# A masked softmax of four cross-attention layers: both halves of the last layer's mask on VectorE, and a new order of work

## The chip, the core and the metric

One core of a Trainium2 chip runs the whole program in one launch. The metric is the device time of that launch in microseconds (us), the median of several runs. Five engines take part: TensorE (PE in the profile, with its weight loads as PEld), VectorE (DVE), ScalarE (ACT), GpSimd (POOL) and SyncE (SP), which here only starts transfers. Matrix products land in PSUM, in banks of 512 float32 per partition. GpSimd touches no bank in this kernel, so that whatever it works on has been brought to SBUF by VectorE or ScalarE first.

## The reference

32 sequences of 64 rows by 256 pass through four attention layers. The last one has a self-attention (called C in the kernel), a cross-attention (F) and an MLP (H); its masked scores are what the change is about.

```
def attention(q, k, v, mask):
    scores = jnp.einsum('bhqd,bhkd->bhqk', q, k) / jnp.sqrt(jnp.float32(HD))
    scores = scores * mask - 10000.0 * (1.0 - mask)
    probs = jax.nn.softmax(scores, axis=-1)
    return jnp.einsum('bhqk,bhkd->bhqd', probs, v)
...
ctx = merge_heads(attention(split_heads(q), split_heads(k), split_heads(v), ltor_mask))    # C
x = hidden_states + ctx @ w_ao + b_ao
...
ctx = merge_heads(attention(split_heads(q), split_heads(k), split_heads(v), cross_mask))   # F
x = x + ctx @ w_co + b_co
x = x + gelu(layernorm(x, ln3_s, ln3_b) @ w1 + b1) @ w2 + b2                               # H
```

The mask acts in two halves: a factor (mask / 4, since the head size is 16) and a summand (10000 * mask - 10000). There are 16 heads of 64 by 64 scores for each sequence.

## The kernel before

Two sequences share the 128 partitions, so there are 16 pairs (index i). Each pair passes through stages with letters: N, Q, A and D are the first layer (norm, queries, scores with softmax, transposes and values), K the projections of the context, B the second layer, E and G the third layer's attention and MLP, C, F and H the fourth layer. W are products of a constant tile with itself whose result nobody reads. They keep TensorE at work: WARM_UP of them at the head of the program, IDLE_WORK at its end, once the last pair has left the first layer. S is the setup.

Every stage is a generator for each engine (`pe_c`, `dve_c`, `pool_c` and so on). The table ORDER holds one string for each engine; each letter advances that stage's generator by one step, and `weave` writes the program out in that order. The order of every engine's queue is thus fixed ahead, letter by letter, and pairs overlap: while one is in A, others are in B to H. BANK gives, in the order of TensorE's fills, which of 7 banks each fill uses. `fill_bank` makes TensorE wait until the bank's last user has released it (semaphore free), `wait_fill` makes a reader wait for the fill (full), and `release` marks the instruction that frees the bank.

An attention of C or F goes so. TensorE fills four banks with a quad of heads each (L684, 256 columns of a bank). VectorE multiplies each by the factor, from the bank into the SBUF tile p (L1170 in C, L1219 in F), which releases the bank. GpSimd adds the summand in SBUF, for 8 heads at a time (`pool_attention`, L824), two instructions for one stage. VectorE then takes the maximum (L754), subtracts it (L759), ScalarE raises to the exponential (L788), TensorE transposes (L698), VectorE sums (L763), and the product with the values follows (L711). B and E mask in another way and aren't touched. GpSimd's other large work is scaling the first layer's probabilities (L587) and spreading keys (L815).

Of the kernel before, what the change touches and what calls it, by code (L numbers as in the profile page):

```python
# [10 lines left out]
ALU = mybir.AluOpType  # L11
# [4 lines left out]
NSEQ, S, D = 32, 64, 256  # L16
# [46 lines left out]
WARM_UP = 32  # L63
IDLE_WORK = 68
# [18 lines left out]
def transpose_fills():  # L83
    fills = []
    for u, j, n in units():
# [24 lines left out]
        "nkbsssbnssssfnssskndsnfbedndnkednnebknybfdnneefkfnenekydybbnbnekfkfdydnnkbynefnkbddnynenkfdykdffeybnbnednnkdfn"  # L110
        "ybkyfnbennbeefbkydnfkfeydyyyy"),
    "pe": (
        "wwwwwwwwwwwwwwwwwwwwwwswwwknwsnkswwwwwwqqnasnaakkkskdkddadndddaaddsdnsddaaddddqddqaadddkkdkddnanadbkdbddbndddd"
        "adadddbbabdndbaekeeddeeddqddddqaddekebeenanaedbebaddkgdkggndddggbbaabdcdbncecedccdddaadedecdcdcecdqqddfaddfdfd"
        "eeeenanbefbfdefdkkfkaagkkgddgkhgngbdddkhhckhhcccbbacbdddnbaddeaacececdddcedeqddfddddfqfddeeeebnaanefbfefdkdkka"
        "agfkgdggngdddbadhdcdkhndkcchccbkbabddcbkehecaaceddcddeheddqfddddfqfddeebeenanefafefbkfkkaagkkkggnddgghbdhkkhdc"
        "hnhcbccbddcabddddbaddeaaddeecdcdececqqddfddddfdfdeeeebanenafefbaafgkgdfgkkggnhkkdhbddkhckkcccddcadbhdbddabddcn"
        "hbddceaaceecddeeddfdddfdqfddeebeeanqebffaafedkfkkangkkgbdggngdhdkhhcbnhcccbhcddbaaddbkdkecdcddaacedecddededddf"
        "dddfqfddqneeeeaneffafbekfkkbdaagdkgggdgdkkbddhnkckhchchchacdbbdddnbaddcbcdeaaceeddcdeeddqfdddfdafddqneebeednae"
        "fbfefdkkagfdgkgkdknggbddaahkkhchndddbccdbcbddcadbkhhcedcaaceedcededddfdddfqfddqeeeennaefbfefbkfkkaaakkgkgdgdgh"  # L120
        "dnghbdkkchnccchddcabbddbddbhcceaddaacdededcededdfdddfdqfddqeeeenaeffnfebkkkaagbkfnkggdbdgkdgdhkaddchbckcbhchha"
        "cbddddbaddnccaaeddecdedeceqddfdddfdfddqnebeeeanaefbfefdkkfkagkkngbdkggnhgadhcdkccbchbcddbaadhchdbcddekddaacdee"
        "ddcdeeddfddddfdfqqdeeebenanaebffedfdkkfgaakgghndkggbdkhcnhckkcbcbddcaabdhbdhedkcdcddaacdedecddeeddfdddfdqfddee"
        "beeaqnebffefanaagkfgkdgdkgkghbddknkkhchcnccbddbcaabdhbhdedcdkcddaacedddedceeddqqdfdddfddfebenneebefafefkkfkaaa"
        "kdgkgdgdhggkhbdkchcccddcaabhhdbkcddcdbcbddecaaedfedfdfdeeddddddfffkkddkeebkbefebwwekhehhgkbbgbgbgegeeewwweckcc"
        "chkcweeewehwecwwecwwwcwwgcggfggfwwfwwwcwwwccwwwfccfwwwfkfcwwcwwwcwwwwchwwwhfwwwfwwfhhhffwwwwfwwwwfwwwwwwwwwwwh"
        "wwwhhhh"),
# [12 lines left out]
    "dve": (  # L140
        "nnsknkknnknnnsnnnsnasansaaskaksfaaakndanadnanaaandnsdaanasnananankddaaabkaakakddaaadnaaannanakdadbbbbbabbdbbab"
        "bdbannneaananaabadbnnaaeendaneaeeeeeddaeadekeaenaannaneaaegbgggbbbgdbbkbkabbdangnbbgbagnacccakcndabnbcanacadec"
        "cnakeccccaaccecnccadcdaacnecfeffaeefeeadfdaffefeefdnfeffaffeffafeagfdgkgngfhahgaahnhknagagkdnabgncccbnbebcbnbb"
        "hhkbbkabbbfchcacccadcncadaabccacacnccacneennacakdacffdfeeaefeekedfdeffeffdefefnaafffaefffaaegngkfggdbgannaaakf"
        "gagahnhhgdachnnccbbbcbnbabdfabnbhdbcbcbkabhncceccnccaacccbccanecakanckadkeackaffdaffeeeeedehfdeffdfeefefnfafff"
        "efffakengfagaggfaghhaakanangfangkhdbenhgabcnbbbbnbcckhcbhbbbnbnabhdncccccakacckddcabancaccaaadeccecaadnaceecff"
        "feaefebeddfeffdfefefeafknfafefaaegffggfgangaafagnkfahegnhhahagcnfcknchbbabdbbcbkbhbckbcdbbccbcakcadcncdnccckan"
        "aahcnnbckncnaaadceaaeacfdfafeefeeedfedffedfefefafeffnfaefffbaaaefagkgagfghhgankeaangbabhbnbgbbhbbngnbcccncnbhd"
        "bbdahckcncchccccaacncbnaaadnckcdacncakaeckafaaedcfaffdefeeeedfedffeffeefnffefnkfffdfaeakfaaeggfageghgaafahagdg"
        "hbnankgdcckahcbbbbncbnbbbnbkhahbcncbbhacccacdccdcancaacbccnacnananckeaeadcafdkffaeefeeeedfdaaffffedeanefffekff"  # L150
        "ffefaaegggfgnagdankfhaghghnedbkhgabbbcnbcbcbbcabnkbnabnbhbaanhacddacccnccaccnabcncchkccnacfkadaeceaakcafdffaee"
        "feeedfedfffefeefdffkeffnffenfaakefgaggngfaahgakabahnkghhgaannanndgcccbhbfcdbbknahbcbbcbkbnebbbcccacnccdccabcdc"
        "cncaaahnaaacedaaeakcfdfkfaeefeeedfedffefefefeffffnffdfaenkaegggfggaananknafbaghghbabbbbhbbnkhgcddcacbcbbfbaaeb"
        "kakhchcnnhaccccadcdccacabnacccacanadnbnenkaaecdakcfffeeaefeeefddffeffdefenffaaenffaefffaeagfgggknfgahnaakhhngb"
        "abbbbbnhgnknnbbdfngcccbcahebbdccabcchccnaccacnccccahcdbndaaakkakaaceaeaadcfffdbaefeeeedfefdffefdeeffneafaffafe"
        "kffaaeggggfngkfanahahdhngahgnkaangnabccbcnbbcbbdbbbbnhbbcchkecnfccacacaacdbccaccdnnkcncaahacbeaaeacdffdfkaefee"
        "eedfedffedffeefafeffffeffakegnggagafagnaakafhkhhggdaaahkngbcncbcbnnnbnbbcbbbdfbaehbccnkhbccnacccaccbaancdccabd"
        "cnhcknaaakeaacdeadckfffaeeeeefeeddfedfffefeeffefkfffeffkanafnegfahggaagegkahaahgahdgagccafchbcbdbbbhbcbcbbbkcc"
# [102 lines left out]
def build(nc, dram, out):  # L261
    ctx = ExitStack()
    with ctx:
# [897 lines left out]
        def dve_c(i):  # L1161
# [7 lines left out]
            def masked(ps, dst):  # L1169
                return dve.tensor_tensor(dst, ps, bc(self_mul[:, :], 1, HB // 2), ALU.mult)  # L1170
# [399 lines left out]
```

## Time and profile before

| | us |
|---|---|
| median of 3 runs | 1190.07 |
| the 3 runs | 1190.07, 1185.77, 1190.25 |
| the profiled execution's own time | 1190.05 |
| its span | 1188.3 |
| PE busy | 1177.5 (99%) |
| DVE busy | 943.5 (79%) |
| ACT busy | 843.8 (71%) |
| POOL busy | 636.4 (54%) |

The profile was taken in one execution. Its own time is 1.75 us above its span, for what lies before the first and behind the last instruction. "Busy" of PE counts matmuls whose ends are modelled, so that a busy PE also holds small pauses between groups. A time in the sections below is counted from the start of the span.

### The profile page before, as it was taken

What the parts mean: (1) busy time and instruction counts of PE and PEld (TensorE: products, weight loads), DVE (VectorE), ACT (ScalarE), POOL (GpSimd) and SP (SyncE); (2) the same over time, 40 slices, a digit from 0 to 9 for tenths busy, and PEclk for the clock granted to TensorE, in tenths of its full rate; (3) what the DMA queues carried; (4) which work ended last, traced back from release to release, by engine and by line L of the source; (5) the groups of instructions that cost most, each with busy time, mean ns of one, the idle gap of its engine ahead of it and who ended that gap; (6) DMA issues with size and microseconds to landing.
All of it is one profiled execution on the core that took longest, in us unless ns stands there. A gap on an engine that the chain in (4) does not pass through costs nothing.

```text
span 1188.3 us, 35233 instructions
## 1 busy us (share of the span) xinstructions
PE 1177.5 (99%) x13192; PEld 973.2 (82%) x13192; DVE 943.5 (79%) x2282; ACT 843.8 (71%) x2273; POOL 636.4 (54%) x1003
## 2 busy tenths in 40 slices
PE   9999999999999999999999999999999999999998
PEld 8777788887887879888787887878888787888887
DVE  4788787978878787787969788797887979788764
ACT  3777786776777677687777868677686776866543
POOL 1654664646465464645656466464654555373341
PEclk8999999999999999999999999999999999999999
DMA  7400000000100000010000000010000100000000
GB/s 240 153 19 29 2 26 12 28 3 7 30 7 20 18 20 14 7 31 7 26 1 11 27 17 25 1 34 6 8 21 1 28 16 2 13 6 2 1 6 10
DMA packets 27623, 27.90 MB, mean 23 GB/s; under 512 B 11073, under 2 KB 25409, under 8 KB 26817
## 3 DMA queue, kind: packets, MB, share of 16 engines
q1 hardware_dynamic: 26240, 24.99, 6.9%
q8 instruction: 109, 1.79, 0.6%
q10 hardware_dynamic: 1216, 0.66, 0.3%
q14 instruction: 58, 0.47, 0.1%
HBM read 23.53 MB, written 2.10 MB: 22 GB/s over the span
## 4 chain that ended last, share of the span: by engine, by line
PE 95%; DVE 2%; ACT 1%; issue 1%; POOL 0%; POOLq 0%; ACTq 0%; DVEq 0%
PE bank L540 10%; PE bank L660 10%; PE attended L615 10%; PE bank L952 10%; PE bank L600 10%; PE bank L962 9%; PE bank L698 6%; PE bank L666 6%; PE bank L725 5%; PE bank L684 4%; PE bank L711 4%; PE bank L511 3%; PE bank L653 3%; PE bank L434 2%; PE attended L1255 2%; PE bank L716 1%
## 5 line engine op out<-in xcount | busy, mean ns | idle before, releaser
L587 POOL TENSOR_SCALAR p_a<-p_a,rec_a 128x256 f32<-128x256 f32 x512 | 246.0, 495 | 121.3 <-DVE rec_a L561 117.9
L576 ACT ACTIVATE p_a<-bank,nmax_a 128x256 f32<-128x256 f32 x512 | 237.3, 475 | 48.8 <-DVE nmax_a L555 47.8
L555 DVE TENSOR_REDUCE nmax_a<-bank 128x2 f32<-128x512 f32 x256 | 170.4, 679 | 15.3 <-PE bank L540 14.0
L600 PE MATMUL bank<-ident,p_a 128*128 128x128 f32 x1024 | 143.0, 275 | 0.3 <-POOL p_a L587 0.2
L540 PE MATMUL bank<-cc,q_a 64*128 64x256 f32 x1024 | 133.0, 390 | 0.4
L600 PEld LDWEIGHTS bank<-ident,p_a 128*128 128x128 f32 x1024 | 116.2, 142 | 17.2 <-issue 10.8
L615 PE MATMUL attended<-p_a,v_a 128*64 128x256 f32 x1024 | 125.8, 386 | 0.2 <-DVE p_a L633 0.2
L540 PEld LDWEIGHTS bank<-cc,q_a 64*128 64x128 f32 x1024 | 93.6, 186 | 24.6 <-issue 12.9
L576 ACT ACTIVATION_READ_ACCUMULATOR p_a<-bank,nmax_a 128x1 f32 x512 | 105.6, 206 | 0.0
L615 PEld LDWEIGHTS attended<-p_a,v_a 128*64 128x64 f32 x1024 | 67.2, 136 | 43.5 <-issue 14.6
L633 DVE COPY p_a<-bank 128x512 f32<-128x512 f32 x128 | 86.3, 679 | 7.3 <-PE bank L600 6.8
L648 ACT ACTIVATE p_a<-bank 128x512 f32<-128x512 f32 x128 | 75.7, 599 | 20.9 <-PE bank L600 20.2
L952 PE MATMUL bank<-h_xnT,wc 128*128 128x128 f32 x512 | 62.2, 276 | 0.5 <-ACT h_xnT L907 0.5
L952 PE MATMUL bank<-g_xnT,wb 128*128 128x128 f32 x512 | 61.7, 276 | 0.0
L952 PEld LDWEIGHTS bank<-h_xnT,wc 128*128 128x128 f32 x512 | 59.9, 192 | 1.7 <-ACT h_xnT L907 1.2
L952 PEld LDWEIGHTS bank<-g_xnT,wb 128*128 128x128 f32 x512 | 59.7, 192 | 0.8 <-ACT g_xnT L907 0.2
L962 PE MATMUL bank<-wc,h_hid 128*128 128x256 f32 x256 | 59.8, 380 | 0.0
L962 PE MATMUL bank<-wb,g_hid 128*128 128x256 f32 x256 | 59.7, 381 | 0.0
L523 ACT ACTIVATE q_a<-bank,bq 128x512 f32<-128x512 f32 x64 | 42.3, 686 | 24.0 <-PE bank L511 23.8
L844 POOL TENSOR_TENSOR b_p<-b_p,b_rec 128x512 f32<-128x512 f32 x32 | 33.6, 1053 | 46.3 <-DVE b_rec L766 46.3
L1136 POOL TENSOR_TENSOR e_p<-e_p,e_max 128x1024 f32<-128x1024 f32 x26 | 49.2, 1901 | 13.4 <-DVE e_max L754 13.3
L824 POOL TENSOR_TENSOR c_p<-c_p,self_add 128x512 f32<-128x512 f32 x32 | 41.8, 1311 | 20.0 <-DVE c_p L1170 19.9
(262 smaller groups left out, 2893.5 us busy)
## 6 DMA issues: line engine op xcount, KB each, us to landing
xx<-in_x SPq DMA_DIRECT2D x32, 128.0 KB, 2.8
cc<-in_ctx SPq DMA_DIRECT2D x32, 128.0 KB, 2.7
wc<-in_wc SPq DMA_DIRECT2D x3, 1024.0 KB, 12.1
k_c<-in_ctx SPq DMA_DIRECT2D x16, 128.0 KB, 2.3
wb<-in_wb SPq DMA_DIRECT2D x2, 1024.0 KB, 6.2
res_a<-in_x SPq DMA_DIRECT2D x16, 128.0 KB, 2.4
out<-y_out SPq DMA_DIRECT2D x16, 128.0 KB
wb<-in_wb SPq DMA_DIRECT2D x2, 512.0 KB, 4.9
```

Of the source, the lines that this page charges most:

```text
L540: ins = mm(bs[e][:, qt * D:(qt + 1) * D], q_a[rows_, j, n, qt * P:(qt + 1) * P], cc[rows_, z, n, :], start=True, stop=True)
L555: dve.tensor_reduce(nmax_a[:, n, e, :], ps[:, :].rearrange("p (q k) -> p q k", q=KT), AX.X, ALU.max, negate=True).then_inc(A.s["max"], 1)
L576: last = act.activation(p_a[:, j % 2, n, e, qt, :], ps[:, qt * D:(qt + 1) * D], ACT.Exp, bias=nmax_a[:, n, e, qt:qt + 1], accum_out=sum_a[ ...
L587: last = pool.tensor_scalar(p_a[:, j % 2, n, e, qt, :], p_a[:, j % 2, n, e, qt, :], rec_a[:, n, e, qt:qt + 1], 1.0, ALU.mult, ALU.mult)
L600: last = nc.tensor.transpose(ps[:, kt * D + qt * P:kt * D + (qt + 1) * P], p_a[:, j % 2, n, e, qt, kt * P:(kt + 1) * P], ident[:, :])
L615: last = mm(attended_bank[n * S:(n + 1) * S, 0:D], v_a[:, n, kt, h * S:(h + 1) * S], p_a[:, j % 2, n, e, kt, :], start=h == 0 and kt == 0, ...
L633: release(A, dve.tensor_copy(p_a[:, j % 2, n, 1, :, :], ps[:, :].rearrange("p (k q) -> p k q", k=KT)), i, ("x", u, 1))
L648: release(A, act.activation(p_a[:, j % 2, n, 0, :, :], ps[:, :].rearrange("p (k q) -> p k q", k=KT), ACT.Copy), i, ("x", u, 0))
L660: last = mm(ps[:, m * P:(m + 1) * P], w[:, k, m * P:(m + 1) * P], srcT[:, k, :], start=k == 0, stop=k == KT - 1)
L666: last = mm(ps[:, 0:D], srcT[:, k, :], w[:, k, :], start=k == 0, stop=k == KT - 1)
L952: last = mm(ps[:, m * P:(m + 1) * P], W["w1"][:, k, cols_], T.xnT[:, k, :], start=k == 0, stop=k == KT - 1)
L962: last = mm(ps[:, 0:D], T.hid[:, m, :], W["w2"][:, m, :], start=m == 0, stop=m == MT - 1)
```

## The change

In C and F, VectorE now does both halves. For each quad it multiplies the bank by the factor and writes the result back to the same place in the bank (line 746 of the changed kernel), raising a semaphore `weighed`; then it adds the summand, from the bank into SBUF (L1167 in C, L1215 in F), and this second instruction releases the bank. The product of the next quad is written ahead of the sum of this one. GpSimd's addition is gone, and the maximum waits for the release of the bank, where it waited for GpSimd before.

```
-RAISED_C = {"res": 1, "madd": KT, **SOFTMAX, **NORM}
+RAISED_C = {"res": 1, "weighed": QUADS, **SOFTMAX, **NORM}
...
-        def dve_attention(T, i, masked, dst):
+        def dve_attention(T, i, masked, dst, weight=None):
             dve, blocks = nc.vector, T.blocks
             for g in range(QUADS):
                 yield
+                if T in (C, F):
+                    for later in range(g, min(g + 2, QUADS)) if g == 0 else range(g + 1, min(g + 2, QUADS)):
+                        yield
+                        ps = wait_fill(T, dve, i, ("s", later))
+                        scores = ps[:, 0:D].rearrange("p (h k) -> p h k", h=HB // 2)
+                        dve.tensor_tensor(scores, scores, bc(weight[:, :], 1, HB // 2), ALU.mult).then_inc(T.s["weighed"], 1)
+                yield
+                if T in (C, F):
+                    dve.wait_ge(T.s["weighed"], T.at(i, "weighed", g + 1))
                 ps = wait_fill(T, dve, i, ("s", g))
...
-                if T is C or T is F:
-                    dve.wait_ge(T.s["madd"], T.at(i, "madd", r + 1))
-                else:
-                    written(T, dve, i, ("s", quads_of(r)[-1]))
+                written(T, dve, i, ("s", quads_of(r)[-1]))
...
-        def pool_attention(T, i, mask_add, mask_ready):
-            pool = nc.gpsimd
-            for r in range(KT):
-                yield
-                mask_ready(pool)
-                written(T, pool, i, ("s", quads_of(r)[-1]))
-                v = heads_of(T, r)[:, 0, :, :]
-                pool.tensor_tensor(v, v, bc(mask_add[:, :], 1, HB), ALU.add).then_inc(T.s["madd"], 1)
...
             def masked(ps, dst):
-                return dve.tensor_tensor(dst, ps, bc(self_mul[:, :], 1, HB // 2), ALU.mult)
-            yield from dve_attention(C, i, masked, x4[:, :])
+                return dve.tensor_tensor(dst, ps, bc(self_add[:, :], 1, HB // 2), ALU.add)
+            yield from dve_attention(C, i, masked, x4[:, :], self_mul)
```

F is changed in the same way. All five strings of ORDER and the string BANK are replaced, and the numbers of W steps with them:

```
-WARM_UP = 32
-IDLE_WORK = 68
+WARM_UP = 30
+IDLE_WORK = 79
...
-        "nkbsssbnssssfnssskndsnfbedndnkednnebknybfdnneefkfnenekydybbnbnekfkfdydnnkbynefnkbddnynenkfdykdffeybnbnednnkdfn"
+        "nskbssbnssssfnsssksknnfnedddekenfndbnbneynfdbkenfydbdnkynedbnenkbnfknynfnykdeyndbknfedyefnbkfnfndkenbbeykbdnfn"
...
```

The first place is VectorE's queue at the last pair's F, from the first product of the scores; f_p is the tile p of F, h_hid the hidden layer of H for the pair ahead. Before:

```order
L1219 TENSOR_TENSOR f_p<-bank,m_mul 128x256 x4
L928 TENSOR_TENSOR h_hid<-bank,cols 128x512
L754 TENSOR_REDUCE f_max<-f_p 128x8
L759 TENSOR_TENSOR f_p<-f_p,f_max 128x512
L754 TENSOR_REDUCE f_max<-f_p 128x8
L759 TENSOR_TENSOR f_p<-f_p,f_max 128x512
```

And now:

```order
L746 TENSOR_TENSOR bank<-bank,m_mul 128x256 x2
L1215 TENSOR_TENSOR f_p<-bank,m_add 128x256
L746 TENSOR_TENSOR bank<-bank,m_mul 128x256
L1215 TENSOR_TENSOR f_p<-bank,m_add 128x256
L746 TENSOR_TENSOR bank<-bank,m_mul 128x256
L1215 TENSOR_TENSOR f_p<-bank,m_add 128x256
L925 TENSOR_TENSOR h_hid<-bank,cols 128x512
L1215 TENSOR_TENSOR f_p<-bank,m_add 128x256
L760 TENSOR_REDUCE f_max<-f_p 128x8
L765 TENSOR_TENSOR f_p<-f_p,f_max 128x512
L760 TENSOR_REDUCE f_max<-f_p 128x8
```

Where four products stood ahead of the hidden layer's bias, the four products and three of the four sums stand now, with the last sum behind it; the two maxima and subtractions follow as before.

The second place is TensorE's queue near the end of the program, from the scores of C for pair 14, while the last pair is in E (e_p, e_v, e_yT). The rows with mean_of_all are W steps. Before:

```order
L684 MATMUL bank<-c_kblk,c_qT 64x128 x16
L1255 MATMUL attended<-mean_of_all 128x128
L698 MATMUL bank<-ident,e_p 128x128 x12
L1255 MATMUL attended<-mean_of_all 128x128
L698 MATMUL bank<-ident,e_p 128x128 x4
L962 MATMUL bank<-wc,h_hid 128x256 x4
L1255 MATMUL attended<-mean_of_all 128x128
L711 MATMUL bank<-e_p,e_v 32x64 x32
L716 MATMUL bank<-ident,e_qT 128x128 x2
L698 MATMUL bank<-ident,c_p 128x128 x4
L1255 MATMUL attended<-mean_of_all 128x128 x2
L725 MATMUL bank<-wb,e_yT 128x256 x2
```

And now:

```order
L685 MATMUL bank<-c_kblk,c_qT 64x128 x16
L699 MATMUL bank<-ident,e_p 128x128 x4
L1250 MATMUL attended<-mean_of_all 128x128 x3
L699 MATMUL bank<-ident,e_p 128x128 x12
L1250 MATMUL attended<-mean_of_all 128x128 x5
L712 MATMUL bank<-e_p,e_v 32x64 x32
L717 MATMUL bank<-ident,e_qT 128x128 x2
L1250 MATMUL attended<-mean_of_all 128x128 x5
L726 MATMUL bank<-wb,e_yT 128x256 x2
L699 MATMUL bank<-ident,c_p 128x128 x8
```

E's transposes (e_p) are cut at another place, H's second half (L962) has left the stretch for an earlier place, and there are more W steps in its stead. Over the program there are 109 W steps where there were 100.

The third place is TensorE's queue in mid program, from the scores of C for pair 6, with what each instruction waits for (free2 is the release of bank 2, b_scaled the scaled probabilities of B). Before:

```order
L684 MATMUL bank<-c_kblk,c_qT 64x128 [waits free5,free6,free2,free0,c_kblk]
L684 MATMUL bank<-c_kblk,c_qT 64x128 x15
L600 MATMUL bank<-ident,p_a 128x128 [waits free3,a_prob]
L600 MATMUL bank<-ident,p_a 128x128 x3
L698 MATMUL bank<-ident,b_p 128x128 [waits free2,b_scaled]
L698 MATMUL bank<-ident,b_p 128x128 x3
L698 MATMUL bank<-ident,b_p 128x128 [waits free5,b_scaled]
```

And now:

```order
L685 MATMUL bank<-c_kblk,c_qT 64x128 [waits free6,free1,free2,free4,c_kblk,free5]
L685 MATMUL bank<-c_kblk,c_qT 64x128 x15
L601 MATMUL bank<-ident,p_a 128x128 [waits free0,a_prob]
L601 MATMUL bank<-ident,p_a 128x128 x3
L699 MATMUL bank<-ident,b_p 128x128 [waits free2,b_scaled]
L699 MATMUL bank<-ident,b_p 128x128 x3
L601 MATMUL bank<-ident,p_a 128x128 [waits free0,a_prob]
```

In both, the second fill behind the scores asks again for bank 2, which holds the first quad of these scores, and stands only one group of four transposes behind them. Before, bank 5 (another quad's) is asked for right after that; now a bank that isn't among the four (bank 0) comes in between.

## Rows read from the trace of the kernel before

**Rows 1.** The page: span, busy time, slices of a fortieth, and the chain.
```profile
span 1188.3 us, 35233 instructions
PE 1177.5 (99%) x13192; PEld 973.2 (82%) x13192; DVE 943.5 (79%) x2282; ACT 843.8 (71%) x2273; POOL 636.4 (54%) x1003
...
PE   9999999999999999999999999999999999999998
...
DVE  4788787978878787787969788797887979788764
...
POOL 1654664646465464645656466464654555373341
PEclk8999999999999999999999999999999999999999
...
PE 95%; DVE 2%; ACT 1%; issue 1%; POOL 0%; POOLq 0%; ACTq 0%; DVEq 0%
```

**Rows 2.** TensorE's waits: for whom, us in total, times, longest.
```profile
PE attended L1255 <- POOL minus_half L1261: 1.0, 1, 1.0
PE bank L711 <- ACT f_p L795: 0.8, 1, 0.8
```

**Rows 3.** Windows: length, busy us of PE, PEld, DVE, ACT, POOL; clock.
```profile
200.00:800.00 600.00, 599.52 (x6891) 494.20 (x6881) 494.37 (x1200) 445.69 (x1207) 344.12 (x530) 1.00 0.06 17
1050.00:1189.00 139.00, 130.79 (x1530) 111.23 (x1528) 95.45 (x218) 70.64 (x156) 53.10 (x80) 1.00 0.02 6
```

**Rows 4.** Groups by line and form: busy us, mean ns, idle before.
```profile
L824 POOL TENSOR_TENSOR c_p<-c_p,self_add 128x512 f32<-128x512 f32 x32 | 41.8, 1311 | 20.0 <-DVE c_p L1170 19.9
...
L824 POOL TENSOR_TENSOR f_p<-f_p,m_add 128x512 f32<-128x512 f32 x32 | 40.5, 1274 | 21.1 <-DVE f_p L1219 21.0
...
L1255 PE MATMUL attended<-mean_of_all 128*128 128x128 f32 x200 | 31.1, 304 | 1.0 <-POOL minus_half L1261 1.0
...
L759 DVE TENSOR_TENSOR c_p<-c_p,c_max 128x512 f32<-128x512 f32 x32 | 24.6, 768 | 0.5
...
L1219 DVE TENSOR_TENSOR f_p<-bank,m_mul 128x256 f32<-128x256 f32 x64 | 24.1, 413 | 1.2 <-PE bank L684 1.0
L1170 DVE TENSOR_TENSOR c_p<-bank,self_mul 128x256 f32<-128x256 f32 x64 | 23.9, 416 | 22.4 <-PE bank L684 22.2
...
L759 DVE TENSOR_TENSOR b_p<-b_p,b_max 128x512 f32<-128x512 f32 x32 | 22.0, 687 | 0.3
```

**Rows 5.** Line 1170 alone: shortest, median and longest, ns.
```profile
L1170 DVE TENSOR_TENSOR c_p<-bank,self_mul x64: 370/415/426, 133.3 to 1147.8; 128x256 f32<-128x256 f32 x64
```

**Rows 6.** VectorE in order of time at the last pair's F.
```profile
1163.99 1.42 DVE L1219 TENSOR_TENSOR f_p<-bank,m_mul 128x256 f32<-128x256 f32 x4 [0.21 <-PE bank L684]
1165.96 0.69 DVE L928 TENSOR_TENSOR h_hid<-bank,cols 128x512 f32<-128x512 f32 x1 [0.55 <-PE bank L952]
1166.57 0.68 DVE L754 TENSOR_REDUCE f_max<-f_p 128x8 f32<-128x512 f32 x1
...
1168.60 0.69 DVE L759 TENSOR_TENSOR f_p<-f_p,f_max 128x512 f32<-128x512 f32 x1
```

**Rows 7.** GpSimd, then ScalarE, in order of time at the same place.
```profile
1164.89 2.50 POOL L824 TENSOR_TENSOR f_p<-f_p,m_add 128x512 f32<-128x512 f32 x2 [5.57 <-DVE f_p L1219]
...
1168.63 1.33 ACT L788 ACTIVATE f_p<-f_p 128x512 f32<-128x512 f32 x2
```

**Rows 8.** The chain in order of time: start, us, what.
```profile
67.11 0.87 PE bank L600 x8
...
70.80 1.02 PE bank L600 x8
...
1165.92 3.46 PE bank L962 x16
...
1170.01 0.66 PE bank L698 x4
...
1170.67 0.89 PE attended L1255 x8
```

More of the change, by code:

```diff
@@ new lines @@
+        "eqenebffefanaagkfgkddgkgkghbdknhcdkkchnccbddcbaabddhbhddcekcddaaceedddcdeeddqqdfdddfddfebebneeneaffefkkkfaaakk"
+        "gkggdghdghbdkcdhcccddcabhadbhddcckdbcbddcaeaefedfdfdeddedddddfffkddkfkeebkbeewbwwekhehkhgbbgbgbgegeekeecwwwcch"
+        "hccewwweeewwwwwewwwwweccwwwcwwwgcgggfgfwwfkcwwwccwwwwfccfwwwfkwwwwwcfcwwwcwwwwchwwwhfwwwfwwfhhhfwfwwwfwwwwfwww"
+        "wwwwwwwwhwwwhhhh"),
+    "act": (
+        "skkqqqnanasqaadaadkaakaaddaaaddaqaaqqqaaddkaaknkaabdnabdabddbaabbabadaeakadaqeqddeqqeaeabeeenaaendbaagbbdggaab"
+        "bdkabcadcaaeadacdccecacaqqdfadqeaeqneeeebfneffbfafadkkkgaagdgaahbhckhbdbckbabadaacecaccacddaaeqfqddeqqeeeeebnf"
+        "aaebfffndfakkkagaagdgaachbadbkdahcbbhcbcaeakccacadaadfeqdqedeqeeqeenbfaeffnffabkkakagaagdgakhkbhchabdbdbcbaadc"
+        "aacedaacdcecaafqqddeeqeeqeenaebfanfabffafgaagkkgdkhakcdbakbchhddbabacabcacdceacaadafdedqeeqenebeeaaefbfqffqafa"
+        "dkkakngakaghgbhbcdahbcbbaacdcdaceakcacadadeafddeqeqqneqeefenfffeafabkakadkbgaagdkghacbkhhbacdabdbabccaaeccdaca"
+        "daaefdqdqeaeaqnqeebeenfeffbdfafagkkkggdakaahbadcbabdacbhhbadckaccceacadaafeddeqqeqeeqeennfefffbfaakkbkaagaagdg"
+        "khahkcbabdhcabbcdbdcaecaacacadadafdedeqeqneeeefqfqeffnaafbkkkabdgaakgdgbhkabhcaahaacbddbcbcaacceaadcdaeadfqqde"
+        "qqeebenaeefaeffbfnafakkkgadakggdhbbcaabkcbhbhadcadcaceacaacddaaefddeqqeqneeebeqfaaefbffanfdagkkkaaghgadkbcbahh"
+        "cbbkbadcacdaaeccacaadadfeddeqeqebeeqeafefbffafnqnaagkaagkkgadhdacbkbhcbkhbbdaccadecaacaacdadaeqqdfqdqeebeeneen"
+        "fefbffafakkkaagaagkghdaadcbbhkhcabacdbcccabdcaeaafadadfedfdfffkekkbeebeeeehbkbgbbgbhgeechkeeeceeeecccccgggfcff"
+        "fcffccccchkfhhfffffhhh"),
@@ L190, in fill_places @@
+    "51460312503145206321456305635261430521054236150423650146501246510243513024651120142065124036512430650124650120"
+    "4651046531026543106245")
 def fill_places():
@@ L230 @@
 RAISED_E = {"m_in": 32, "mask": 1, "res": 1, "kblk_own": 1, **SOFTMAX}
-RAISED_C = {"res": 1, "madd": KT, **SOFTMAX, **NORM}
-RAISED_F = {"m_in": 16, "mask": 2, "res": 1, "madd": KT, **SOFTMAX, **NORM}
+RAISED_C = {"res": 1, "weighed": QUADS, **SOFTMAX, **NORM}
+RAISED_F = {"m_in": 16, "mask": 2, "res": 1, "weighed": QUADS, **SOFTMAX, **NORM}
 RAISED_G = {"res": 1, **NORM, "msq": 1, "hid": 2}
@@ L1181, in pool_c @@
             yield from pool_spread(C, i, 0, C, "k", "kblk")
-            yield from pool_attention(C, i, self_add, lambda pool: ready(pool, i))
             yield from pool_wide(C, i)
@@ L1218, in masked @@
             def masked(ps, dst):
-                return dve.tensor_tensor(dst, ps, bc(m4_mul[:, :], 1, HB // 2), ALU.mult)
-            yield from dve_attention(F, i, masked, x5[:, :])
+                return dve.tensor_tensor(dst, ps, bc(m4_add[:, :], 1, HB // 2), ALU.add)
+            yield from dve_attention(F, i, masked, x5[:, :], m4_mul)
         def dve_h(i):
@@ L1237, in pool_f @@
             yield from pool_norm(F, i, 0)
-            yield from pool_attention(F, i, m4_add, lambda pool: pool.wait_ge(F.s["mask"], F.at(i, "mask", 2)))
             yield from pool_wide(F, i)
```

126 lines of the change are left out of this document (55 added, 71 removed).

## The prediction, made before the changed kernel was run

> **What bounds the kernel now.** I read the page's busy shares first, then TensorE's waits, then windows, then single places at the end. TensorE is busy for 1177.5 of 1188.3 us, and its slices stand at 9 from first to last but one, at a granted clock that is full (2.4 GHz) in every slice but the first; the chain is 95% TensorE [rows 1]. From 200 to 800 us it is busy for 599.52 of 600 us [rows 3]. Its longest wait anywhere is 1.0 us, at the very start, the next is 0.8 us [rows 2]. So in mid program TensorE's own work sets the pace, and no other engine's speed counts as long as it isn't late. The reader is to see that VectorE, with 494.37 of those 600 us, has 105.6 us free, and GpSimd more [rows 3]. Only the end is different: from 1050 us TensorE is busy for 130.79 of 139 us [rows 3], and many of those are W steps that compute nothing. There the last pairs' chain through VectorE, ScalarE and TensorE sets the time.
>
> A profiled execution took 1190.05 us, 1.75 above its span, and the median of the runs is 1190.07, so that sums against the one serve for the other. The three runs lie between 1185.77 and 1190.25.
>
> **GpSimd's part.** Removed are 32 + 32 additions at 1311 and 1274 ns, 82.3 us of GpSimd's time [rows 4]. Nothing of TensorE's waited for GpSimd beyond 1 us [rows 2], so this gives 0 directly.
>
> **VectorE's part.** Added are 4 instructions for each C and F, 8 for a pair, 128 in all. The product changes its target from SBUF to the bank, the sum is new. Neither form is in the trace; the nearest row is the old product, from a bank into SBUF, same shape: 416 and 413 ns [rows 4], between 370 and 426 [rows 5], and four in a row take 1.42 us, 0.355 each [rows 6]. I take 0.355 for each step in the queue, 45.4 us in all, and 128 x 0.414 = 53.0 us of busy time. Bounds for the pair of instructions: below, 0.355 each; above, the 0.69 of an instruction with twice the columns [rows 6] for the one in place, which would add another 128 x 0.335 = 42.9 us. The wait on `weighed` costs nothing where another product stands between product and sum, which it does for each quad but the last, whose product is two sums ahead.
>
> A small gift: the subtraction in C takes 768 ns on average against 687 in B, at the same shape [rows 4]; in C it runs while GpSimd adds the second half of the heads, in B no such addition exists. 32 x 81 ns = 2.6 us of VectorE's time may return. The Trainium skill says why, on the page "SBUF — State Buffer", section "Who interferes with whom": a VectorE instruction with two inputs in SBUF contends with a GpSimd instruction that reads SBUF. The rows agree with it; it doesn't enter the sum, since VectorE is off the path.
>
> So VectorE goes from 943.5 to about 994 us busy, 83 to 84%. In mid program its load rises by 53.0 x 600/1188 = 27 us in 600, and of 105.6 us free some 79 remain. What hides it is TensorE's unbroken work on other pairs. If that cover were gone, the 45.4 us would be paid whole, at 1235.5 us; the new order is there to keep it. I take 0, and bound it at 0.4 us for each of the 32 stages, 12.8 us, by the rival below.
>
> **The banks.** This is the new constraint. Before, with products back to back, the four banks came free 0.41, 0.77, 1.12 and 1.48 us after the first product began. Now VectorE's row is product, product, sum, product, sum, product, sum, sum; the sums that free the banks are third, fifth, seventh and eighth, so 1.12, 1.83, 2.54 and 2.90 us [rows 6]. In the order's third place, in pair 6, TensorE asks for the first quad's bank again behind one group of four transposes, half of 0.87 us [rows 8], thus 0.44 us. Before, 0.41 was just in time; now it is 0.7 us late. I laid the steps' durations end to end along both orders for all 32 such stages: this is the only one where the bank is asked for sooner than VectorE can give it; the first quad's bank is asked for again after 1.9 us in the median of C (1.0 before) and 2.8 in F (2.3 before), an estimate from chain rows of the groups. Term: +0.7 us. The Trainium skill, page "PSUM — Partial Sum Buffer", "Summary: rules for kernel authors", speaks against the change: "Evacuate promptly — 2 MiB is tight". No row here shows a wait for a bank; by that rule the slower rival would hold.
>
> **The W steps.** 109 of them stand in the program for 100. Eight records, four steps, take 0.89 us in the chain [rows 8], 0.222 each. The eleven more at the end cost 2.4 us if TensorE's queue is what ends last there, the two fewer at the start give 0.4 us back.
>
> **The end of the program.** Here the mask work is on the chain. Take the last F. First product at 1163.99, first maximum at 1166.57, behind the hidden layer's bias [rows 6]; GpSimd's two additions from 1164.89 took 2.50 us, to 1167.39 [rows 7], and were hidden by that bias and the first maximum. In the new queue (first place) seven instructions at 0.355 end at 1166.48, the bias takes 0.61 more, and the last sum 0.41: the first maximum begins at 1167.5, 0.9 us later. The second subtraction began at 1168.60, the second exponential ended at 1168.63 + 1.33 = 1169.96 and the transposes that need it began at 1170.01, in the chain [rows 6 to 8]. TensorE's 3.46 us of H's second half, until 1169.38 [rows 8], covers only what comes before. So +0.9 us here. Four such stages lie in the end stretch (C and F of the last two pairs), between 0 and 0.9 us each: 0 to 3.6. GpSimd's removed additions shorten none of them by more than this already contains. The longer chain and the eleven W steps fill the same time and aren't added to each other: 2.4 us for both, which is 4 x 0.6. The order's second place shows it: 13 W steps stand in the rows where 5 stood, with four of H's products among them.
>
> **Start.** The same chain of loads, statistics, norm and queries; the loads of the columns have moved ahead of the context's. I take only the two W steps, -0.4, between -1 and +1.
>
> **Sum.** 1190.05 + 0.7 + 2.4 - 0.4 = 1192.75; I say 1192.7 us, +0.2%. A change within 0.5% (1184.1 to 1196.0) is about what a measurement of this kernel can't tell from none.
>
> **Rivals.**
>
> 1. VectorE late (slower). Mechanism: each C and F holds VectorE 1.42 us longer and the four banks longer. Behind it in VectorE's queue stand the first layer's maxima, which ScalarE and GpSimd and then TensorE's transposes wait for. If the instruction in place costs more than 0.355 us, or the order leaves less room than I count, TensorE loses time in each of 32 stages. It decides from about 0.25 us a stage, since 8 us and the 2.7 of the forecast pass 1196.0. At 0.4 us it is 12.8, and 1192.7 + 12.8 = 1205.5 us. For it: no margin was left before in pair 6, and VectorE stands at 83% in mid program with a fixed order. Against it: at that load TensorE lost 0.48 us in 600, and the banks are asked for later by the new order. Chance 0.20, with small cases reaching down to 1197.
>
> 2. The new order packs TensorE better (faster). Groups of the same eight transposes take 0.87 us in one place and 1.02 in another [rows 8], 0.15 us lost in a hand-over that counts as busy. If 40 such are gone, 6 us: 1192.7 - 6 = 1186.7; to pass 1184.1 it takes 58. For it: GpSimd, with 82 us less work, finishes the scaled probabilities sooner, and these transposes wait for them. Against it: the program has as many groups as before, within half a percent. Chance 0.14, of which 0.07 under 1184.1.
>
> 3. The end is no longer (no change). TensorE has 8.2 us without work from 1050 us on, about 3 of them behind its last product [rows 3], and the W steps replace some of the rest. With the start's -0.4 that gives 1190 us. Chance 0.14.
>
> 4. The exchange of engines doesn't keep TensorE busy enough at the end and the granted clock falls to 1.2 GHz there. It stayed full through this end stretch with W steps in it [rows 1, 3]. Chance 0.01, counted with rival 1's side.
>
> The forecast has 0.51, with its own range of 1190 to 1196. The range for 8 in 10 takes rivals 2 and 3 and the lower part of rival 1: 1186.5 to 1200.5. Faster: 0.07. Slower: 0.20 from rival 1, 0.01 from rival 4 and nothing of the forecast, 0.21. Within 0.5%: 0.72.
>
> **What would show it.** VectorE busy 985 to 1000 us, GpSimd near 554; the product in place near 415 ns; C's subtraction near 690. TensorE still above 99.7% busy from 200 to 800 us. W steps x218 by records. The end, from the last product of the first layer on, 2 to 3 us longer. Wrong would be: an instruction in place well above 0.45 us; TensorE waiting for VectorE or for a bank in mid program by more than a few us in all; a span below 1184, which would need faster groups in mid program.

## The result, and the profile after

The changed kernel takes 1201.31 us, the median of 3 runs (1197.61 to 1201.6), against 1190.07 (1185.77 to 1190.25). The ratio is 1.0103, 95% interval 1.0079 to 1.0127. It is slower by 11 us; the prediction, 1192.7 with a range of 1186.5 to 1200.5, missed.

Both kernels have two levels, 4 us apart, which the three runs of each show already. In 62 runs beside the experiments the kernel before took 1185.8 to 1186.6 us (28 runs, the lower level) with a granted clock of 1.0 over the span, or 1189.9 to 1190.6 (31 runs, the upper level) with 0.997, and three lay in between. Two windows show where the levels part, the first from the kernel before on the upper level, the second from the first experiment below, which has the same order, on the lower: on the lower level TensorE's clock was full from 10 to 20 us, on the upper it was 0.66 in the mean there, and TensorE began 71 matmuls in place of 121. Two runs, at 1576.03 us in experiment 5 and 1216.95 in experiment 10, had clocks of 0.75 and 0.95 and are left out where levels are compared. From here on, kernels are compared at equal level. After against before that gives 1201.4 - 1190.3 = 11.1 us on the upper level, and 1197.6 - 1186.1 = 11.5 on the lower, where the changed kernel has one run.

```profile
10.00:20.00 10.00, 9.38 (x71) 7.92 (x72) 4.20 (x20) 1.19 (x3) 1.26 (x2) 0.66 0.84 276
```
```profile
10.00:20.00 10.00, 9.38 (x121) 7.52 (x114) 4.97 (x18) 3.92 (x8) 1.26 (x2) 1.00 0.79 257
```

The page of the changed kernel, beside [rows 1]:

```profile
span 1199.9 us, 35434 instructions
...
PE 1187.1 (99%) x13210; PEld 973.7 (81%) x13210; DVE 976.1 (81%) x2410; ACT 852.9 (71%) x2277; POOL 551.1 (46%) x939
...
PE   9999999999999999999999999999999999999998
...
PEclk8999999999999999999999999999999999999999
...
PE 93%; DVE 5%; issue 1%; ACT 1%; POOL 0%; POOLq 0%; DVEq 0%; ACTq 0%
```

TensorE's "busy" grew by 9.6 of the 11.5 us that the span grew, though it got only 18 matmuls more, all of them W steps. Its waits hardly grew against [rows 2]:

```profile
PE bank L712 <- issue: 1.1, 2, 0.8
PE attended L1250 <- POOL minus_half L1256: 1.1, 1, 1.1
PE bank L699 <- DVE c_p L1167: 0.7, 1, 0.7
```

The windows, columns as in [rows 3]:

```profile
200.00:800.00 600.00, 597.69 (x6819) 488.60 (x6804) 508.56 (x1256) 449.46 (x1199) 297.88 (x492) 1.00 0.06 16
1050.00:1189.00 139.00, 134.35 (x1583) 112.69 (x1584) 107.08 (x252) 74.58 (x172) 42.65 (x73) 1.00 0.02 6
```

The reader is to see the counts in brackets. In the same 600 us TensorE began 6819 matmuls where 6891 stood before, 1% less work, and was "busy" for 99.6% all the same. The ends of matmuls are modelled, so short gaps between them count as busy, and a TensorE that gets less done in a busy microsecond looks like one at its limit. (The count is a rough measure, since matmuls differ in length and a different mix may fall into the window.) The loss is spread over mid program: the last of the first layer's matmuls into the attended bank begins at 1079.1 us before and at 1088.5 after, and of the 11.5 us of span 9.4 lie ahead of it and 2.1 behind.

VectorE's groups, beside [rows 4] (mean in ns after the comma):

```profile
L746 DVE TENSOR_TENSOR bank<-bank,self_mul 128x256 f32<-128x256 f32 x64 | 25.8, 423 | 15.3 <-PE bank L685 15.2
...
L1167 DVE TENSOR_TENSOR c_p<-bank,self_add 128x256 f32<-128x256 f32 x64 | 25.3, 411 | 0.0
...
L765 DVE TENSOR_TENSOR c_p<-c_p,c_max 128x512 f32<-128x512 f32 x32 | 22.2, 694 | 0.4
```

The product in place costs 423 ns in C and 421 in F (404 to 433), 7 or 8 more than the old product into SBUF, and the sum 411 and 404.

### The profile page after: what moved, and what is told of

The parts are those of the page before. It is cut to its first block, busy times and chain, and to the rows that moved or that the text cites. A ratio compares the mean times of both kernels' runs of the same rounds, so it can differ in the third digit from the quotient of the medians.

```text
span 1199.9 us, 35434 instructions
## 1 busy us (share of the span) xinstructions
PE 1187.1 (99%) x13210; PEld 973.7 (81%) x13210; DVE 976.1 (81%) x2410; ACT 852.9 (71%) x2277; POOL 551.1 (46%) x939
## 4 chain that ended last, share of the span: by engine, by line
PE 93%; DVE 5%; issue 1%; ACT 1%; POOL 0%; POOLq 0%; DVEq 0%; ACTq 0%
PE bank L541 11%; PE bank L661 10%; PE attended L616 10%; PE bank L601 9%; PE bank L949 9%; PE bank L959 9%; PE bank L699 6%; PE bank L667 5%; PE bank L726 5%; PE bank L685 4%; PE bank L712 4%; PE bank L512 3%; PE bank L654 3%; PE bank L435 3%; PE bank L717 1%; PE attended L1250 1%
## 5 line engine op out<-in xcount | busy, mean ns | idle before, releaser
L959 PEld LDWEIGHTS bank<-wc,h_hid 128*128 128x128 f32 x256 | 46.9, 190 | 6.0 <-ACT h_hid L976 0.5
L959 PEld LDWEIGHTS bank<-wb,g_hid 128*128 128x128 f32 x256 | 46.9, 190 | 5.5
```

The costliest lines, as they stand in the source:

```text
L959: last = mm(ps[:, 0:D], T.hid[:, m, :], W["w2"][:, m, :], start=m == 0, stop=m == MT - 1)
```

## A measure that "busy" does not give

Since busy time hides the loss, I added up TensorE's time from the start of one matmul to the start of the next, in every trace, and sorted the intervals by the tile that a matmul uses (rows x columns of the array, as the rows name it: 128*128, 64*128, 128*64, 32*64 or 128*32). A form is such a tile. Three facts come out, the same in each kernel's trace:

- Within one form an interval depends on the shape alone: 109 to 111 ns for 128 moving columns (the columns that a matmul sends through the tile), 215 to 216 for 256; a 64*128 matmul of 256 costs 209 from the last of one step to the next step's first.
- Where the next matmul has another form, the interval is 94 to 97 ns longer: 109 becomes 203 to 205, 215 becomes 309, 209 becomes 306, 422 becomes 520.
- The step behind the change also takes longer than among its like: eight 64*128 matmuls take 0.86 us between two steps of the same form, 0.96 to 0.97 with another form on one side, 1.06 with another on both; four transposes 0.44, and 0.49 when the form changed ahead of them. So coming into 64*128 costs 104 ns, and into 128*128 about 50 (55 for a step of two or four matmuls, 37 for one of eight, some 15 for one of sixteen), on top of the 96 for leaving. No 128*64 step follows its like, but two of eight matmuls take 0.15 us more than one of sixteen, which is again 96 and some 50. Into 32*64 and 128*32 no cost is counted.

TensorE changes form 474 times in the order of before and 504 times in the new one. The table splits the stretch from 60 us to the last matmul into the attended bank (us, all worked out from the traces): "own" is every matmul by its interval within a form, "form" the changes by the three prices, "rest" what is left, in the main waits for data and banks too short for the waits view, and what the three prices miss. The work in the stretch is the same in every row but for a few W steps, so "own" should be too. It varies by 1.1 us, and the split is no finer than that.

| kernel | stretch | own | form (changes) | rest | behind it, to the end |
|---|---|---|---|---|---|
| before | 1018.8 | 951.1 | 61.6 (424) | 6.1 | 109.2 |
| after | 1028.5 | 950.9 | 66.7 (454) | 10.9 | 111.3 |
| new order, one VectorE instruction | 1027.2 | 950.7 | 66.7 (454) | 9.8 | 109.7 |
| old order, the edit | 1040.8 | 951.3 | 61.8 (425) | 27.7 | 112.8 |
| before, 15 steps moved, 30 more changes | 1024.7 | 951.5 | 66.6 (455) | 6.6 | 109.2 |
| before, 25 steps moved, as many changes | 1022.3 | 951.8 | 61.8 (425) | 8.7 | 109.1 |

## The experiments

**1 to 4: the order and the edit apart.** The first keeps before's order and does the mask in one VectorE instruction a quad, without GpSimd's additions:

```
-                return dve.tensor_tensor(dst, ps, bc(self_mul[:, :], 1, HB // 2), ALU.mult)
+                return dve.scalar_tensor_tensor(dst, ps, HD ** -0.5, bc(self_add[:, :], 1, HB // 2), ALU.mult, ALU.add)
...
-                pool.tensor_tensor(v, v, bc(mask_add[:, :], 1, HB), ALU.add).then_inc(T.s["madd"], 1)
```

> The order, the banks and the W steps of the kernel before; GpSimd's additions are gone and VectorE masks each quad of C and F with one scalar_tensor_tensor (a quarter of the score plus the summand), as many VectorE instructions as before. For masks of 0 and 1 the softmax comes out the same. It measures what GpSimd's part was worth. Theory L (VectorE's added work makes TensorE late): 1190 us, ratio 1.000, since TensorE's pace is untouched. Theory O (the new order itself packs TensorE worse): the same. Rival that GpSimd's additions cost something: below 1186.

Measured: 1186.33 us (1185.89 to 1190.19), ratio 0.999 [0.9977, 1.0004]. At equal level it is 1186.3 against 1186.4 and 1189.9 against 1190.3. GpSimd's 82 us are worth some tenths at most, and both theories stand.

The second puts the edit alone into before's order, banks and W steps (the next quad's product in the same step as this quad's sum):

```
+                    for later in ((0, 1), (2,), (3,), ())[g]:
+                        ...
+                        dve.tensor_tensor(scores, scores, bc(weight[:, :], 1, HB // 2), ALU.mult).then_inc(T.s["weighed"], 1)
+                    dve.wait_ge(T.s["weighed"], T.at(i, "weighed", g + 1))
```

> The edit alone: both halves on VectorE with the product in place in the bank, in the order, the banks and the W steps of the kernel before (each quad's step holds the product of the next quad and the sum of this one). Theory L: VectorE is late by some tenths of a us in each of 32 stages in an order that wasn't laid out for it: 1200 to 1212 us, at least as slow as the changed kernel's 1201.3. Theory O: 1190 to 1194 us, since the order is the old one and VectorE has room.

Measured: 1215.38 us (1211.75 to 1215.49), ratio 1.0227 [1.0206, 1.0248], 25 us slower. TensorE's waits, its window and the chain of this run:

```profile
PE bank L600 <- DVE c_p L1169: 2.7, 5, 0.7
PE bank L698 <- DVE c_p L1169: 1.9, 3, 0.9
PE bank L434 <- DVE f_p L1218: 1.7, 2, 0.9
```
```profile
200.00:800.00 600.00, 594.23 (x6744) 484.94 (x6744) 500.02 (x1245) 437.50 (x1188) 291.63 (x489) 1.00 0.06 15
```
```profile
PE 84%; DVE 9%; issue 4%; ACT 1%; POOL 1%; POOLq 0%; DVEq 0%; ACTq 0%
```

Now TensorE waits by name for the sums of C and F (L1169 and L1218), and the table's rest is 27.7 us. Theory O, with its 1190 to 1194, falls for the old order, and theory L had the loss too small. VectorE being late is real, in the old order.

The third takes the new order and its banks with the light mask: the products are gone, the sum is experiment 1's instruction.

```
-                        dve.tensor_tensor(scores, scores, bc(weight[:, :], 1, HB // 2), ALU.mult).then_inc(T.s["weighed"], 1)
...
-                return dve.tensor_tensor(dst, ps, bc(self_add[:, :], 1, HB // 2), ALU.add)
+                return dve.scalar_tensor_tensor(dst, ps, HD ** -0.5, bc(self_add[:, :], 1, HB // 2), ALU.mult, ALU.add)
```

> The changed kernel's order, banks and W steps, with its products in place left out and each sum replaced by one scalar_tensor_tensor (a quarter of the score plus the summand), so that VectorE has 128 instructions and about 50 us less work. Theory L: the loss goes with the work, 1191 to 1194 us (the nine W steps stay). Theory O: the loss stays, 1198 to 1201 us. In between, both have a share in proportion.

Measured: 1198.93 us (1198.8 to 1199.03), ratio 1.0096 [1.0078, 1.0115]. All its runs are on the upper level, so against experiment 1 on that level (1189.8 to 1190.2): +9.0 us, and against before (1190.3) +8.6. The time lies in theory O's range. The new order with its W steps makes about four fifths of the loss of 11.1 us; VectorE's 128 extra instructions add the other 2.5 (1201.4 - 1198.9).

The fourth is the changed kernel with the product written to SBUF, which releases the bank, and the sum within SBUF:

```
+                        release(T, dve.tensor_tensor(part, ps[:, 0:D].rearrange("p (h k) -> p h k", h=HB // 2), bc(weight[:, :], 1, HB // 2), ALU.mult), i, ("s", later))
...
+                    dve.tensor_tensor(part, part, bc(summand[:, :], 1, HB // 2), ALU.add).then_inc(T.s["weighed"], 1)
```

> The changed kernel with the same number of VectorE instructions in the same places, but the product goes from the bank to SBUF and releases the bank, and the sum is made within SBUF. Rival B (the banks are held too long): 1192 to 1196 us. Theory L and theory O: no change from the changed kernel, 1199 to 1203 us; a sum within SBUF may contend with GpSimd and be somewhat longer.

Measured: 1206.51 us (1205.84 to 1206.85), ratio 1.0159 [1.0141, 1.0178]: 5 us slower than after though the banks come free sooner, and outside the range of either side. The early release has a price here: the sum within SBUF costs 461 ns in C and 498 in F, against 411 and 404 out of the bank, 9 us more for the 128 of them:

```profile
L751 DVE TENSOR_TENSOR f_p<-f_p,m_add 128x256 f32<-128x256 f32 x64 | 31.3, 498 | 0.0
L751 DVE TENSOR_TENSOR c_p<-c_p,self_add 128x256 f32<-128x256 f32 x64 | 28.5, 461 | 0.0
```

**5 and 6: light engines in either order.** The two kernels with one VectorE instruction a quad (experiments 1 and 3) are taken again. The first layer's maxima, GpSimd's scaling in the first layer and in B, and the gelus touch only a part of their columns and leave the rest undone; all of TensorE's work stays:

```
-                    dve.tensor_reduce(nmax_a[:, n, e, :], ps[:, :].rearrange("p (q k) -> p q k", q=KT), AX.X, ALU.max,
+                    dve.tensor_reduce(nmax_a[:, n, e, :], ps[:, :].rearrange("p (q k) -> p q k", q=KT)[:, :, 0:32], AX.X, ALU.max,
```

> The kernel with one masking instruction a quad in the order of before (1190 us at the level of the head that the profile of before has), and the other engines made lighter: the first layer's maxima read 32 of 256 keys, GpSimd scales 32 of 256 keys there and 8 of 64 in B, and the gelus touch an eighth of the hidden layer; all of TensorE's work stays. Some 120 us go from VectorE, 180 from GpSimd, 50 from ScalarE. It sets the floor for TensorE's queue in this order. If small waits for other engines are part of the time, it falls to 1175 to 1185 us; if TensorE's queue alone sets it, it stays at 1188 to 1190.

> The same lightening in the order of the changed kernel, with one masking instruction a quad. Theory O1 (the new order loses 7 us because its hand-overs leave the other engines too little time): the difference of 8.9 us to the old order shrinks to about the nine W steps, 2 us. Theory O2 (the loss is in TensorE's own queue, in how its groups follow one another): the difference stays at 7 to 9 us however light the others are.

Measured: 1187.74 us in the old order, 0.9988 [0.9974, 1.0002], and 1197.89 in the new, 1.0079 [1.0063, 1.0096]. At the upper level 1188.6 and 1197.9: 9.3 us apart, as with full engines (9.0), so that theory O1, with its 2 us, falls. The order's loss doesn't hang on how long these instructions take. The exponentials and the copies out of the banks were left as they are.

**7 and 8: without the W steps of the end**, in either kernel:

```
-                mm(attended_bank[:, 0:P], mean_of_all[:, :], mean_of_all[:, :], start=True, stop=True)
+                if n < WARM_UP:
+                    mm(attended_bank[:, 0:P], mean_of_all[:, :], mean_of_all[:, :], start=True, stop=True)
```

> The kernel before without the 68 W steps of its end; those of the head stay. If the W steps only fill time in which TensorE waits, the time is unchanged (1190 at the level of the profile of before); if they are in the way, it falls by up to 68 x 0.222 = 15 us; if the clock falls without them, it rises by tens of us.

> The changed kernel without the 79 W steps of its end. If the W steps only fill, unchanged at 1201. If my term of 2.4 us for eleven more of them holds, the difference of the changed kernel to the one before shrinks by 2 to 3 us against old_no_w. The mid-program loss that the trace shows before the last pair leaves the first layer (10.6 us) must stay in either case.

Measured: 1194.69 (1193.58 to 1195.95), 1.0054 [1.0035, 1.0073], and 1206.07 (1199.33 to 1207.56), 1.0134 [1.0107, 1.0161]. The medians rise by some 5 us and stay 11 apart, but the runs spread: 1193.6 and 1195.9 in the old order, 1199.3 and 1206.1 in the new. Neither kernel gets faster, so the steps aren't in the way. Without them TensorE is thin at the end and the clock can fall, here from 1150 to 1190 us in before's order (0.79 after the last bracket; it stood at 1.00 with them); in the two runs at 1199.3 the clock was 0.999 over the whole span, so it hardly fell. The loss of mid program stays, as expected: the last product into the attended bank begins at 1079.0 and 1088.4 us.

```profile
1150.00:1190.00 40.00, 29.88 (x234) 24.14 (x234) 18.10 (x45) 15.40 (x27) 8.34 (x13) 0.79 0.01 4
```

**9 and 10: changes of form put in on purpose.** Two kernels differ from before only in TensorE's order (and its banks' list, moved along). One of the 15 moves of the first, as the order of instructions shows it (a matmul here is two in the trace):

```
 L698 MATMUL bank<-ident,c_p 128x128 x4
-L653 MATMUL bank<-ident,x 128x128 x2
-L540 MATMUL bank<-cc,q_a 128x256 x8
+L540 MATMUL bank<-cc,q_a 128x256 x4
+L653 MATMUL bank<-ident,x 128x128 x2
+L540 MATMUL bank<-cc,q_a 128x256 x4
 L711 MATMUL bank<-c_p,c_v 32x64 x16
```

> The kernel before with nothing changed but TensorE's order: 15 steps between 75 and 1040 us are taken one to three places earlier, each at a moment at which its data and banks had been ready for 0.4 us or more in the trace of before, so that TensorE changes the form of its matmul tile 504 times in place of 474, as often as the changed kernel does. Theory F (a change of form costs TensorE 94 to 97 ns, read off the starts of successive matmuls): 30 x 0.096 = 2.9 us later than before at equal level (a run at full clock from the start 1189.2 against 1186.3, the other 1193.1 against 1190.2). Theory S (the 96 ns are a price of what stands there anyway and overlap hides them, or the changed kernel's loss is waits alone): within 0.7 us of before.

> The control for the run beside it: the kernel before with 25 steps of TensorE taken one to three places earlier by the same rule (data ready 0.4 us or more before), chosen so that the number of changes of form stays 474. Theory F: no change, within 0.7 us of before at equal level. Theory M (it is moving steps at all, and so the moments at which banks fill and free, that costs): 25 moves cost as much as or more than the 15 of the run beside it, 2 to 5 us.

Measured: with 30 changes more, 1191.91 us (1191.39 to 1195.74), 1.0035 [1.0021, 1.0049]; at equal level 1191.5 against 1186.1 and 1195.6 against 1190.3, so +5.4. With 25 moves and no change more, 1192.58 in the median (most runs on the upper level), 1.0027 [1.0012, 1.0042]; at equal level 1188.7 and 1192.9, so +2.6. None of the theories had the numbers: the control isn't free, and 30 changes cost nearly twice 96 ns each. The table tells the two apart. In the control the rest rises by 2.6 us; the time lost at fills whose bank had come free less than 0.15 us before rises by 1.8 of it. In the other kernel the rest rises by 0.5 us, and the form term by 5.0 of the 5.7 us that its span is longer in the trace (31 more changes fall into the stretch). The place of one move, in before and then in the moved order (start, length, tile, as in [rows 8] but with all matmuls):

```profile
419.84 0.60 PE L698 MATMUL bank<-ident,c_p 128*128 128x128 f32 x4
420.28 0.38 PE L653 MATMUL bank<-ident,x 128*128 128x128 f32 x2
420.59 2.00 PE L540 MATMUL bank<-cc,q_a 64*128 64x256 f32 x16
422.52 0.65 PE L711 MATMUL bank<-c_p,c_v 128*32 128x64 f32 x32
```
```profile
421.55 0.60 PE L698 MATMUL bank<-ident,c_p 128*128 128x128 f32 x4
422.08 1.13 PE L540 MATMUL bank<-cc,q_a 64*128 64x256 f32 x8
423.14 0.44 PE L653 MATMUL bank<-ident,x 128*128 128x128 f32 x2
423.51 1.13 PE L540 MATMUL bank<-cc,q_a 64*128 64x256 f32 x8
424.57 0.65 PE L711 MATMUL bank<-c_p,c_v 128*32 128x64 f32 x32
```

From L698's start to L711's it is 2.68 us before and 3.02 after the move, for the same matmuls: 0.34 us for two changes, of which the three prices give 2 x 0.096 + 0.104 + 0.050 = 0.346. No row shows a gap. Over all of the 600 us from 200 us on this run is as busy as before, with 49 matmuls fewer:

```profile
200.00:800.00 600.00, 599.53 (x6842) 490.68 (x6841) 491.84 (x1194) 442.65 (x1196) 345.44 (x530) 1.00 0.06 16
```

**11: six more W steps at the start of before**, three behind the setup's small products and three ahead of the wait for the first weights:

```
-WARM_UP = 32
+WARM_UP = 38
```

> The kernel before with six more of the idle matmuls at its start, three behind the small setup products and three ahead of the wait for the first weights, where TensorE waited 0.6 us and then ran matmuls of a quarter tile; nothing else moves. Theory C (the two levels of before, near 1186.3 and 1190.2, are one fall of the clock to its lower level from 13.0 to 19.8 us, 6.8 us at half speed, 3.4 us lost, and it comes when TensorE was thin in the stretch ahead of it): more work there keeps the clock up, nearly all runs at 1186.3 to 1186.9, none at 1190. Theory R (the fall comes from something else than what TensorE does there): both levels stay, about one run in two each.

Measured: 1187.35 us (1186.68 to 1188.12, 12 runs), 0.9989 [0.9978, 0.9999]. All twelve have a clock of 1.0; the upper level is gone. The two groups of three begin at 10.2 and 11.4 us. Theory C holds, though the time is above its 1186.3 to 1186.9: the steps themselves cost 1.2 us against the lower level of before, and the gain in the median is 1.7, which is 0.14%, and comes only because half of before's runs are on the upper level.

**12: the edit in the old order, banks released early**, experiment 2 with experiment 4's release:

> The edit alone in the old order, and the banks released early: VectorE writes the product into SBUF and so gives each bank back at the product, and adds the second half in SBUF. Compared with the edit alone in the old order with the product in the bank (1215.4). Theory B (in the old order the loss is banks of the last layer held by 0.4 us per product longer, for which TensorE waits): more than half of the 25 us comes back, 1190 to 1203. Theory V (the loss is VectorE's added 53 us in a queue without room for them, whatever the banks do): 1211 to 1221, the sum in SBUF being no shorter than the one out of the bank.

Measured: 1218.44 us (1215.89 to 1223.45), 1.0256 [1.0231, 1.0281]; at the lower level 1216.4 against 1211.8. Theory B falls here too: releasing the banks early gives nothing back. The sum is longer in this kernel as in experiment 4, so that what the hold alone costs isn't measured; most of the 25 us goes with VectorE's added work.

## Why the prediction was wrong

**The step that failed** is the sum's silence on the new order in mid program. Of it the prediction counted one late bank, 0.7 us, after "I laid the steps' durations end to end along both orders", with one duration for each kind of step. A step has no such one duration: eight transposes take 0.89 us from start to start among their like and 1.02 with another form on both sides, eight 64*128 matmuls 0.86 and 1.06. I had a sight of it, the groups of the same eight transposes at 0.87 and 1.02 us "lost in a hand-over that counts as busy" [rows 8], used it only for the faster rival, and set it aside with "the program has as many groups as before, within half a percent". (From start to start the two are 0.97 and 1.02: the first has another form behind it, the second on both sides.) Groups were the wrong thing to count; changes of form are 6% more. Their term is 66.7 - 61.6 = 5.1 us, worked out with the three prices. The run with 30 changes put in shows such changes as a cause of this size: 5.0 of its 5.7 us of span.

The Trainium skill has the rule: "TensorEngine Tiling (Array Packing)", "Key Properties", says "Mode switching requires drain", that changing the tiling mode empties TensorE first. The runs agree that a switch costs time: 96 ns to leave a form and some 15 to 104 to enter the next.

**The rest of the order**, 9.8 - 6.1 = 3.7 us, is in the main short waits. By each step's semaphores, TensorE's time lost behind banks freed less than 0.15 us before rises from 3.8 to 6.0 us in the new order, and the rise is at banks that ScalarE frees; behind the first layer's matmuls that wait for the attended product just issued it rises from 0.7 to 1.5. The bank that the prediction named came out as said. In pair 6 TensorE's transposes wait 0.72 us for the first sum:

```profile
557.82 0.63 PE L699 MATMUL bank<-ident,b_p 128*128 128x128 f32 x4 [0.72 <-DVE c_p L1167]
```

And "this is the only one where the bank is asked for sooner than VectorE can give it" was nearly right for the 32 stages that it spoke of: TensorE's step begins just behind a late sum of C in three places, 1.0 us in all. What the sum left out are the other banks, asked for within tenths of a microsecond of their release. The control, which loses 2.6 us by moving 25 steps one to three places, shows how little slack there is. Why the new order runs into these waits wasn't taken apart further, and the new order with its added changes of form taken out again wasn't run.

**VectorE.** Products at 423 and sums at 411 ns against my 414; a product in place isn't the dear instruction that I bounded it by. VectorE's busy time rose by 32.6 us, where I had 50. Its durations added up rose by 47.6, from 1079.8 to 1127.4; the page counts once what overlaps, as in a row of such instructions 0.33 us apart, and I had added whole durations. The gift came: C's subtraction fell from 24.6 us [rows 4] to 22.2, and to 22.4 in experiment 1, where nothing but the mask's instructions differs from before. For C the trace thus agrees with the Trainium skill's rule on the shared port ("SBUF — State Buffer", "Who interferes with whom"). F's subtraction fell only from 736 to 729 ns in experiment 1, though its additions are gone as well, and to 684 in the changed kernel; no run explains that.

The added work costs 2.5 us, which I bounded by 0 and 12.8 and took as 0. By the table, after's row against that of the new order with one VectorE instruction, it is 1.1 us of rest in mid program and 1.6 at the end.

**The banks.** The Trainium skill, "PSUM — Partial Sum Buffer", "Summary: rules for kernel authors", asks to evacuate promptly; it was my reason for the slower rival. The runs neither bear it out nor refute it: the early release came with a dearer sum, and the pair made the kernel 5 us slower in the new order and 5 in the old.

**The end** came out as said, 2.1 us for 2.4, but the two terms that I didn't add have unequal parts. The new order with its eleven more W steps alone makes it 0.5 us longer (109.7 against 109.2), VectorE's added work 1.6. In the last F the first maximum now follows the first product by 3.26 us, before by 2.58 [rows 6]: 0.7 where I had 0.9.

```profile
1174.89 0.76 DVE L746 TENSOR_TENSOR bank<-bank,m_mul 128x256 f32<-128x256 f32 x2 [0.21 <-PE bank L685]
...
1177.82 0.41 DVE L1215 TENSOR_TENSOR f_p<-bank,m_add 128x256 f32<-128x256 f32 x1
1178.15 0.67 DVE L760 TENSOR_REDUCE f_max<-f_p 128x8 f32<-128x512 f32 x1
```

**GpSimd** at 0 was right. **Rival 1** had the right side and nearly the right time, 1205.5, by luck: its VectorE holds for the old order, 25 us, and is mostly what the new one avoids. Its threshold was off as well: 1196.0 lies 3.3 us above the forecast, so that 0.1 us a stage would have been enough, not 0.25. **Rival 2** had the right place, hand-overs between steps, with the sign reversed. The account of the 11.5 us of span: changes of form 5.1, short waits in mid program 4.8 (3.7 the order's, 1.1 VectorE's), the end 2.1, and -0.5 of smaller things, of which -0.3 lie ahead of the stretch. The short waits are what the split leaves over, so they are the less certain part.

The signs that I had named to watch couldn't have told me: TensorE was busy for 99.6% of the 600 us where I had asked for 99.7, its waits by name stayed small, the product in place was cheap, and the end came out. Only the count of matmuls in the window shows the loss.

So the new order is a good trade for this edit, 14 us better than the old order with it (1201.4 against 1215.4), and edit and order together are a bad one against leaving the mask as it was.

## To carry to other kernels

When TensorE is 99% busy, count what it does in a window, not how long: matmuls per microsecond and changes of tile form tell what "busy" hides. If an edit comes with a new order, price the order by itself, and test it by itself, since here it was about four fifths of the loss. A sum of step durations needs the price of each neighbourhood, and slack in tenths of a microsecond.

## What the runs showed of the hardware

- A change of TensorE's tile form costs 94 to 97 ns ahead of it and, into 128*128 and 64*128, some 15 to 104 ns behind it, counted as busy; the kernel with 30 changes put in is 5.4 us slower, and the form term is 5.0 of it.
- A VectorE product from a bank into the same bank, 128x256, takes 423 ns, within 10 of one into SBUF; a sum within SBUF of that size takes 461 to 498, one out of a bank 404 to 411.
- The two levels come from the clock, which in the profiled run of before stood at 1.2 GHz from 13.0 to 19.8 us: 6.8 us at half speed are 3.4 of the 4.2 us between them. With six more W steps at 10.2 and 11.4 us it never fell there in 12 runs. Without the W steps of the end it stood at 0.79 from 1150 to 1190 us, and the median rose by 5 us.
